# A two-layer transformer forward on one NeuronCore: VectorE's transposition of GpSimd's inverse blocks moves from the start of a batch's forward substitution into the middle of the preceding batch's

## The reference, cut to what matters

```
s = where(strict, einsum('bihd,bjhd->bhij', k, k) * scale, -inf)
p = softmax over j of s, 0 outside strict
L = p * beta.transpose(0, 2, 1)[..., None]
A = L + eye(T)
u = solve_triangular(A, v.transpose(0, 2, 1, 3), lower=True)
attn = softmax(where(causal, q k^T * scale, -inf))
o = einsum('bhij,bhjd->bihd', attn, u).reshape(B, T, HID)
return o @ Wo
```

## Time and profile before

| | us |
|---|---|
| median of three executions | 821.7 |
| lowest and highest | 819.52 and 824.21 |
| the profiled execution, its own time | 820.95 |
| its span in the trace | 819.1 |
| busy in the span: PE, DVE | 515.0, 555.0 |
| busy in the span: ACT, POOL | 300.3, 227.1 |

### The profile page before, as it was taken

One profiled execution on the slowest core, in us unless ns is written; L12 is line 12 of the kernel. 1 busy time (PEld: TensorE's weight loads), 2 busy tenths in 40 slices (PEclk: granted clock), 3 DMA queues, 4 the chain that ended last, 5 costly groups with the idle time before them and its releaser, 6 DMA issues. The chain is left out here.

```text
span 819.1 us, 17908 instructions
## 1 busy us (share of the span) xinstructions
PE 515.0 (63%) x7444; PEld 424.2 (52%) x7444; DVE 555.0 (68%) x1066; ACT 300.3 (37%) x716; POOL 227.1 (28%) x320
## 2 busy tenths in 40 slices
PE   0362555875859554327565676678886750899980
PEld 0352444764648443325443455466655540899980
DVE  6899699797969847766656684663664165667834
ACT  3354333543456340062654204523213150365520
POOL 3000000000000000104848807816830036043254
PEclk9875775986888786755586666687979555899996
DMA  8445041050000100760070150020001162666224
GB/s 307 149 76 116 1 89 28 1 117 1 2 0 2 52 0 17 159 136 5 3 155 6 40 90 7 7 47 7 10 10 12 55 245 85 245 204 235 78 58 136
DMA packets 52067, 61.30 MB, mean 75 GB/s; under 512 B 25409, under 2 KB 45393, under 8 KB 47505
## 3 DMA queue, kind: packets, MB, share of 16 engines
q1 hardware_dynamic: 50176, 55.15, 25.1%
q0 software_dynamic: 1808, 4.99, 2.0%
HBM read 45.24 MB, written 13.63 MB: 72 GB/s over the span
## 5 line engine op out<-in xcount | busy, mean ns | idle before, releaser
L888 PE MATMUL psum<-arena 32*32 32x16 f32 (+18 forms) x5608 | 357.6, 274 | 214.3 <-DVE arena L1557 75.7
L888 PEld LDWEIGHTS psum<-arena 32*32 32x32 f32 (+6 forms) x5608 | 284.4, 128 | 287.1 <-DVE arena L1557 78.4
L1994 POOL TENSOR_TENSOR arena<-arena 128x31 f32<-128x31 f32 (+15 forms) x124 | 68.4, 552 | 9.7
L1992 POOL TENSOR_TENSOR arena<-arena 128x31 f32<-128x31 f32 (+15 forms) x124 | 64.4, 519 | 9.7
L1350 ACT ACTIVATE psum<-psum,arena 128x256 f32<-128x256 f32 (+7 forms) x128 | 45.7, 364 | 30.4 <-DVE arena L1618 30.2
L1527 DVE TENSOR_TENSOR_SCAN arena<-arena 128x255 f32<-128x255 f32 x64 | 42.5, 726 | 11.4 <-ACT arena L1262 11.4
L1628 DVE TENSOR_REDUCE arena<-psum 128x2 f32<-128x512 f32 (+1 forms) x48 | 41.3, 861 | 12.5 <-PE psum L888 11.8
L1972 POOL DMA_DIRECT2D arena<-wq x1 | 0.9, 862 | 171.9 <-PE psum L888 171.9
L1319 ACT ACTIVATE arena<-psum 128x512 f32<-128x512 f32 (+1 forms) x48 | 35.4, 736 | 35.8 <-PE psum L888 35.5
L2005 POOL TENSOR_TENSOR fc_second_parts<-arena,fc_first_parts 128x2048 fp32r<-128x2048 f32 x6 | 27.9, 4650 | 63.7 <-ACT fc_first_parts L1438 63.7
L1262 ACT ACTIVATE arena<-arena 128x255 f32<-128x255 f32 x64 | 27.2, 498 | 46.6 <-DVE arena L1513 46.6
(11 more groups left out here) (179 smaller groups left out, 928.0 us busy)
## 6 DMA issues: line engine op xcount, KB each, us to landing
arena<-fc SPq DMA_DIRECT2D x16, 1024.0 KB, 5.2
arena<-parts SPq DMA_DIRECT2D x40, 256.0 KB, 4.5
parts<-arena SPq DMA_DIRECT2D x16, 384.0 KB, 3.6
arena<-parts SPq DMA_DIRECT2D x40, 128.0 KB, 5.4
dispatched<-arena SPq DMA_DIRECT2D x1, 2048.0 KB, 18.9
arena<-arena SPq DMA_DIRECT2D x128, 8.0 KB, 1.8
arena<-dispatched SPq DMA_DIRECT2D x8, 256.0 KB, 3.3
expert_rows<-arena SPq DMA_DIRECT2D x8, 256.0 KB, 2.3
```

Of the source, the lines that this page charges most:

```text
L888: return nc.tensor.matmul(out, lhsT, rhs, start=start, stop=stop)
L1992: link(G_.tensor_tensor(tmp, A3[:, k + 1:BLK, k:k + 1].to_broadcast([P, rows, w]), X3[:, k:k + 1, 0:w].to_broadcast([P, rows, w]), ALU.mult))
L1994: ins = G_.tensor_tensor(X3[:, k + 1:BLK, 0:w], X3[:, k + 1:BLK, 0:w], tmp, ALU.add)
```

## The change

The step `inverse` no longer opens the chain of its own batch. Batch 0's stands ahead of all; those of batches 1, 2 and 3 become units of the work that `spread` distributes over the preceding batch's chain, at 3/4, 1/2 and 1/4 of the list `ahead`. `lag()` now starts its mode for the substitution at the first `solve`. No instruction is added or removed, and none changes its shape.

```diff
+    o += [("inverse", 0)]
+    for b, at in enumerate((3 / 4, 1 / 2, 1 / 4)):
+        ahead[b].insert(int(len(ahead[b]) * at), [("inverse", b + 1)])
     for b in range(B):
 
-        solve = [[("inverse", b), ("solve", b, 0, 0), ("solve", b, 0, 1)]]
+        solve = [[("solve", b, 0, 0), ("solve", b, 0, 1)]]
...
-        if step[0] == "inverse":
+        if step[0] == "solve":
             solving = True
```

## The result

The changed kernel takes 823.62 us (median of 20 runs, 821.87 to 829.15), the kernel before, beside it, 819.45 us (20 runs, 816.0 to 824.89). The ratio is 1.0040, with an interval of 1.0023 to 1.0057: 3.3 us slower, between 1.9 and 4.7, which is inside the 0.5% of the prediction but not zero. The profiled execution has a span of 823.0 us, where that of before had 819.1.

The account below looks back on a forecast made before the run. No engine was taken as busy throughout; a TensorE-VectorE chain and GpSimd's inversions run through the substitutions. Terms -0.4 + 0 + 5.0 = +4.6 us on 820.95 or 821.7 gave 826.0 us, range 820.0 to 829.8.

Parts of the forecast that it names:

- rival A: Substitution 2: the wait comes, but the rest makes most of it up; 820 to 824 us, chance 0.26.
- Boundaries, 0: Between batches: removing three transpositions, 5.9 us of VectorE, gains 0, since TensorE covers all three.
- Rival C: Boundaries not covered, giving back up to 5.9 us in all, and the wait vanishes; about 816 us, chance 0.12.
- Substitution 0, -0.4: Transposition 1 makes `minus` end 0.5 us later, shifted units give time back; sum -0.4 us, bounds -1.0 and +1.9.
- Substitution 1, 0: Transposition 2 after `update 1, 3` costs 0, since TensorE reaches `update 1, 4` only at 538.10; bounds 0 and +1.9 us.
- The wait, 4.4 us: Substitution 2: at transposition 3 VectorE stands still 4.4 us for GpSimd's `blocks 3`, reaching `update 2, 2` 5.3 us late.
- The clock, 2.4 us: Substitution 2: TensorE's pause of some 4.5 us halves its clock; `probs 5`, `update 2, 3` and `wo` cost 2.4 us more.
- The net at the last copy, +5.0: Substitution 2's last copy ends at 602.7 us, before 597.74: +5.0, or +2.6 at full clock; bounds -1.0 and +7.7.
- The walk: Following substitution 2's static order from 581.6 us: copy of `solve 2, 4` at 591.2, last copy's end at 602.7.
- Nothing behind the last boundary catches it up: After substitution 2's last copy, `pv 2`, substitution 3 and the output hang on it, so the +5.0 us stays.

Follow-up runs that it names:

- twice_at_starts: The kernel before, with transpositions 1 and 3 each done twice at the start of their batches; +1.2 us beside the kernel before (-1.1 to 3.5).
- filled_wait: The changed kernel, with TensorE writing the first part of `probs 4` of substitution 2 nine times instead of once; +2.3 us beside the kernel before (-0.1 to 4.7).
- early_12: The changed kernel with transpositions 1 and 2 put earlier, at 5/8 and 1/3 of their lists; -1.9 us beside the kernel before (-3.7 to -0.2).
- only_1_2: The changed kernel with only the third transposition put back at its batch's start; -0.3 us beside the kernel before (-2.3 to 1.6).
- early_again: The changed kernel with transpositions 1 and 2 at 5/8 and 1/3 of their lists, measured again; +0.6 us beside the kernel before (-1.7 to 2.9).

## Why the prediction was right, step by step

826.0 us was forecast, in a range of 820.0 to 829.8; 823.62 was measured. The mechanism came as forecast: the third transposition waits for GpSimd, TensorE pauses, and the clock falls behind that pause. In the number there is some luck. 823.62 lies below the forecast's own 824.2 to 829.2 and within rival A's 820 to 824; it is in the stated range because that took in most of A. The forecast also stood on 821.7 us for the kernel before, which measured 819.45 beside the changed one; against that, the measured +3.3 us is inside the +2.5 to +7.5 us of the forecast, and +4.6 would have given 824.1. The sum's terms stand against the profile as follows.

*Boundaries, 0:* right. VectorE's idle time there grew, TensorE is still what ends it, and at the first boundary twice as much work is covered too. Rival C falls with it. That the idle time grows by the whole 2 us is not borne out (1.0, 1.1 and 2.9 us).

*Substitution 0, -0.4:* measured +0.3 from transposition 0 to the first copy of substitution 1 (72.89 against 72.56 us); the shift alone gives -0.2 (72.35), transposition 1 without it +0.9 (73.49). By these I mis-sized both by some half a microsecond, but one profile doesn't tell that much: the eight with this order lie between 72.6 and 73.2 us, and twice_at_starts, which up to its first doubled step does what the kernel before does, takes 2.4 us longer to get there from transposition 0 (65.70 against 63.32).

*Substitution 1, 0:* right (64.88 against 64.94 us). TensorE's stretch from 535.34 covers the transposition. `update 1, 4` came 0.94 us later (539.04 against 538.10), less than the 1.46 us by which the batch's first copy was late.

*The wait, 4.4 us:* it was 3.44. What counts are two lengths from the end of transposition 2: VectorE took 38.50 us to its new place (576.68 less 538.18), where I had 37.85 (575.15 less 537.30), and GpSimd's run took 41.74, where I had taken the longer of two, 42.1. It is the largest of the sizes that I had wrong, by 1.0 us.

*The clock, 2.4 us:* it fell behind a pause of 3.79 us (I had 4.5), and filled_wait prices it at 2.45. The Trainium skill, "TensorE: Matmul & The Clock Gate" (section "HAM oscillation — how this bites in real kernels"), tells of this pattern with a wait for a DMA as the cause; here the trace agrees with a wait for VectorE, and behind it GpSimd.

*The net at the last copy, +5.0:* +3.90 (35.75 less 31.85). The copy of `solve 2, 4` was 5.85 us late, which is 3.44 + 2.45; the transposition's own 1.95 us were hidden, as early_12 shows. The walk had it 6.45 us late there (591.2 less 584.75). From there to the last copy it took 10.77 us against 12.72 before, so 1.95 us came back, where the walk had 1.5. Most of that is the other side of the comparison: in the profile of the kernel before the clock fell in this stretch, and only_1_2, without that fall, takes 11.37 us. Beside only_1_2 the last copy is 5.6 us late (35.75 less 30.11), so +3.90 is good to some 2 us only. One argument of this step was wrong in any case: I put the shifted units down against rival A, because `wo` and `gate` now stand ahead of the copy of `solve 2, 4`. They stood ahead of it before too, and with `wo` in its old place the wait costs +6.7 us, not +3.3. So A had more for it than I gave it.

*"Nothing behind the last boundary catches it up":* not borne out in the profile. `pv 2` ran longer at the lower clock (5.93 us against 5.03), which makes +4.68 at the first copy of substitution 3. Then 2.2 us come back from the start of the last batch's `pv` on: 1.0 in that `pv`, by the clock (see the last section), and 1.2 behind it, which no run here explains. With 1.1 us ahead of transposition 0, where both kernels do the same, and 0.3 in substitution 0, that makes the 3.9 us between the two spans. TensorE's timelines of the last `pv`, of the kernel before and the changed one:

```profile
628.77 0.74 PE L888 MATMUL psum<-arena 98*128 98x256 bf16 x8 [0.29 <-DVE arena L1670]
634.39 5.31 PE L888 MATMUL psum<-arena 128*32 128x256 f32 x64 [4.88 <-DMA arena<-arena]
```

```profile
634.85 0.74 PE L891 MATMUL psum<-arena 98*128 98x256 bf16 x8 [0.29 <-DVE arena L1673]
640.47 4.33 PE L891 MATMUL psum<-arena 128*32 128x256 f32 x64 [4.88 <-DMA arena<-arena]
```

What remains open is how much of these 2.2 us is the change's and how much that of one execution: the fourteen profiles have two lengths up to the end of that `pv`, whatever their order.

## What to carry to other kernels

A consumer moved earlier shortens nothing until its producer's next start is what something waits for: here GpSimd's third run started 20 us sooner (538.35 in place of 558.62), which shortened nothing, and the wait came where its result was now read too early. A step inserted into a chain is free where the other engine has work of its own to do in the meantime (here ahead of `update 2, 3`); where that engine has none and waits (here ahead of the copy of `solve 2, 4`, with `wo` already done), it costs its length and perhaps the clock. And an insertion into a list that is spread evenly moves the other entries too: read each of them in the new order before pricing the one that was meant.

## What had not been expected

The clock does not repeat from one profile to the next. Ahead of the last `pv` TensorE has the same pause of 4.88 us in both kernels, and yet the lower level lasts until about 639.5 us in the kernel before, nearly all of that `pv`, and until about 643.5 in the changed one, some 3 of its 4.3 us. Windows of the kernel before, and of the changed one:

```profile
632.00:634.00 2.00, 0.00 (x0) 0.00 (x0) 0.00 (x0) 0.00 (x0) 0.00 (x0) 0.67 0.14 12
...
638.00:640.00 2.00, 1.70 (x27) 0.91 (x18) 0.00 (x0) 0.20 (x1) 0.00 (x0) 0.62 0.00 0
```

```profile
636.00:638.00 2.00, 0.00 (x0) 0.00 (x0) 0.52 (x3) 1.03 (x3) 0.00 (x0) 0.68 0.03 3
...
642.00:644.00 2.00, 2.00 (x36) 1.40 (x32) 0.00 (x0) 0.00 (x0) 0.00 (x0) 0.62 0.03 8
```

The same products took 5.31 us in one and 4.33 in the other. From the first copy of substitution 3 to the first step behind that `pv` the fourteen profiles take 34.1 to 34.4 us (six of them) or 35.0 to 35.4 (the other eight). The two profiles of one kernel, early_12 and early_again, take 35.06 and 34.11 us there, and 67.36 and 65.78 us for substitution 1. A difference of 1 us between two profiles is therefore no evidence by itself. A set of timed runs can mislead too: the -1.9 us of early_12, clear of zero by its interval, came out as +0.6 the second time.
